# First self attention of a transformer: sixteen piece buffers, two heads built from SBUF, GpSimd as DMA issuer, masked row ahead

## The reference, cut to what matters

```
def _L0_attn_ref(x, wq, wk, wv, wo):
    N_HEADS = 16
    HEAD_DIM = 64
    xq = jnp.einsum('bsh,oh->bso', x, wq)
    xk = jnp.einsum('bsh,oh->bso', x, wk)
    xv = jnp.einsum('bsh,oh->bso', x, wv)
    xq = xq.reshape(bsz, N_HEADS, seqlen, HEAD_DIM)
    scores = jnp.einsum('bhid,bhjd->bhij', xq, xk) * SCALE
    scores = jax.nn.softmax(scores, axis=-1)
    out = jnp.einsum('bhij,bhjd->bhid', scores, xv)
    out = out.reshape(bsz, seqlen, N_HEADS * HEAD_DIM)
    return jnp.einsum('bso,ho->bsh', out, wo)
x = _layernorm(x + _L0_attn_ref(x, wq, wk, wv, wo))
```

## Time and profile before

| what | value |
|---|---|
| median of three runs | 3027.53 us (3024.91 to 3030.15) |
| the profiled execution: its own time | 3025.33 us |
| the profiled execution: its span | 3023.6 us |
| PE busy | 2640.1 us (87%) |
| DVE busy | 1690.4 us (56%) |
| POOL busy | 1567.7 us (52%) |
| ACT busy | 1175.5 us (39%) |
| mean DMA rate | 101 GB/s |

### The profile page before, as it was taken

One profiled execution on the slowest core, in us unless ns is written; L12 is line 12 of the kernel. 1 busy time (PEld: TensorE's weight loads), 2 busy tenths in 40 slices (PEclk: granted clock), 3 DMA queues, 4 the chain that ended last, 5 costly groups with the idle time before them and its releaser, 6 DMA issues. The chain is left out here.

```text
span 3023.6 us, 42611 instructions
## 1 busy us (share of the span) xinstructions
PE 2640.1 (87%) x11953; PEld 1603.7 (53%) x11953; DVE 1690.4 (56%) x3325; ACT 1175.5 (39%) x1640; POOL 1567.7 (52%) x1298
## 2 busy tenths in 40 slices
PE   5999999999999999999999968982795588689696
PEld 4666666666666666666666533431574244334264
DVE  4566666656656566565666535662234455358753
ACT  2444444444444444444444324541222343345334
POOL 0677666776766776676776742224334212222353
PEclk8999999999999999999999979996897599899798
DMA  7545554454545545555454320003893100000143
GB/s 188 119 103 120 113 132 109 112 120 103 120 113 128 112 104 123 112 119 116 111 116 105 75 79 12 2 2 122 343 345 121 39 0 1 29 2 9 33 139 89
DMA packets 406654, 305.26 MB, mean 101 GB/s; under 512 B 291830, under 2 KB 337182, under 8 KB 401438
## 3 DMA queue, kind: packets, MB, share of 16 engines
q1 hardware_dynamic: 390702, 233.93, 33.0%
q0 software_dynamic: 11904, 64.06, 6.0%
q10 hardware_dynamic: 3952, 6.08, 0.6%
HBM read 190.18 MB, written 96.49 MB: 95 GB/s over the span
## 5 line engine op out<-in xcount | busy, mean ns | idle before, releaser
L630 POOL TENSOR_TENSOR a_total<-a_total,a_pr 128x1024 f32<-128x1024 f32 x384 | 915.6, 2384 | 55.8 <-ACT a_pr L614 35.5
L561 DVE TENSOR_REDUCE a_nmax<-a_psX 128x1 f32<-128x512 f32 x1024 | 696.1, 688 | 167.8 <-PE a_psX L556 165.9
L614 ACT ACTIVATE a_pr<-a_psS 128x1024 f32<-128x1024 f32 x512 | 525.3, 1027 | 676.5 <-PE a_psS L602 676.5
L642 PE MATMUL a_psO<-a_pr,a_vd 128*64 128x512 f32 x2048 | 481.8, 602 | 0.0
L556 PE MATMUL a_psX<-a_kA,a_qA 128*128 128x512 f32 x1024 | 411.1, 402 | 30.2 <-DVE a_pl L458 16.2
L630 POOL TENSOR_TENSOR a_total<-a_pr 128x1024 f32<-128x1024 f32 x64 | 153.4, 2398 | 520.2 <-ACT a_pr L614 520.2
L602 PE MATMUL a_psS<-a_qA,a_kA 128*128 128x512 f32 x1024 | 338.4, 412 | 1.6 <-DVE a_nT L577 1.4
L602 PE MATMUL a_psS<-a_qB,a_kB 128*128 128x512 f32 x1024 | 320.4, 394 | 0.7 <-DVE a_qB L585 0.7
L642 PEld LDWEIGHTS a_psO<-a_pr,a_vd 128*64 128x64 f32 x2048 | 129.9, 136 | 236.8 <-issue 179.4
L556 PEld LDWEIGHTS a_psX<-a_kA,a_qA 128*128 128x128 f32 x1024 | 192.9, 189 | 107.5 <-issue 31.8
L602 PEld LDWEIGHTS a_psS<-a_qA,a_kA 128*128 128x128 f32 x1024 | 180.7, 189 | 122.1 <-issue 90.1
(11 more groups left out here) (388 smaller groups left out, 4326.5 us busy)
## 6 DMA issues: line engine op xcount, KB each, us to landing
a_qA<-a_qhi SPq DMA_DIRECT2D x128, 256.0 KB, 4.2
a_qhi<-a_ph SPq DMA_DIRECT2D x128, 128.0 KB, 2.1
a_qlo<-a_pl SPq DMA_DIRECT2D x128, 128.0 KB, 2.2
a_khi<-a_ph SPq DMA_DIRECT2D x128, 128.0 KB, 3.1
a_klo<-a_pl SPq DMA_DIRECT2D x128, 128.0 KB, 2.9
a_kA<-a_khi SPq DMA_DIRECT2D x64, 256.0 KB, 4.0
a_kA<-a_klo SPq DMA_DIRECT2D x64, 256.0 KB, 5.1
a_kB<-a_khi SPq DMA_DIRECT2D x64, 256.0 KB, 5.7
```

What stands on the lines that cost most here:

```text
L561: w.eng.tensor_reduce(nmax[:, half, u:u + 1], psX[:, half, :], AX.X, ALU.max, negate=True)\
L614: w.eng.activation(pr[:, n, :], psS[:, half, :, :].rearrange("p a b -> p (a b)"), ACT.Exp, scale=SCALE)\
L630: w.eng.tensor_tensor(total[:, buf, :], first, pr[:, n, :], ALU.add).then_inc(sems["ad"], 1)
L642: last = w.eng.matmul(psO[q * HD:(q + 1) * HD, :], vd[:, b, kc, :], pr[:, n, q * 512:(q + 1) * 512], start=kc == 0, stop=kc == KC - 1)
```

## The change

Five things are changed in `layer0_self_attention`.

1. `PIECES` goes from 4 to 16: `ph` and `pl` have sixteen buffers, with sixteen semaphores `so0` to `so15`. `build` waits for all of them and for a new one, `sg`.
2. The 16 pieces of group 0 go to DRAM by DMAs that GpSimd issues (32 of them, counted in `sg`), all later pieces by SP as before.
3. The operands of heads 0 and 1 are taken directly from `ph` and `pl` by a new function `build_first`, SBUF to SBUF, in 12 DMAs of 128 KB per head in place of six of 256 KB. ACT waits for these and for `sg` at step 4 of `largest`, before it writes the buffers again.
4. The first weight split stands ahead of the transposition of x.
5. `masked` stands ahead of task "3" at every boundary.

```diff
-    PIECES = 4
+    PIECES = 2 * ROWS // P
...
-        def misc(w, what, G, buf, more=True, bank=None, back=(0, 0)):
+        def misc(w, what, G, buf, more=True, bank=None, back=(0, 0), out="sync"):
...
-                if w.on("sync"):
+                done = f"so{n}" if out == "sync" else "sg"
+                if w.on(out):
...
-                w.inc(f"so{n}", 2 * 16)
+                w.inc(done, 2 * 16)
...
-                w.waits(("s", w.at("s")), *((f"so{n}", w.at(f"so{n}")) for n in range(PIECES)))
+                w.waits(("s", w.at("s")), ("sg", PIECES * 2 * 16), *((f"so{n}", w.at(f"so{n}")) for n in range(PIECES)))
...
+        def build_first(w, j):
+
+            if w.on("sync"):
+                w.wait("md", w.at("md"))
+                for t, rows, src, c, n in ((qA, 0, ph, 0, "a"), (kA, 0, ph, KC, "a"), (qA, HD, ph, 0, "a"), (kA, HD, pl, KC, "a"),
+                                           (kB, HD, ph, KC, "b"), (qB, HD, pl, 0, "b")):
+                    for par in range(2):
+                        w.eng.dma_start(t[rows:rows + HD, j, par * 512:(par + 1) * 512].bitcast(F32).rearrange("p (c t) -> p c t", t=HD),
+                                        src[par * HD:(par + 1) * HD, c:c + KC, j * HD:(j + 1) * HD].bitcast(F32))\
+                            .then_inc(sems[f"f{n}{j}"], 16)
+            w.inc(f"fa{j}", 8 * 16)
+            w.inc(f"fb{j}", 4 * 16)
...
-                rest_first = left > 0 and SLOTS.get((j, "3"), ("T",))[0] in "QK"
-                if more and not rest_first:
+                if more:
                     masked(w, nb)
                 first_d, first_a = under = piece("3")
-                if more and rest_first:
-                    masked(w, nb)
...
             load_x(w, 0)
+            split(0)
             misc(w, ("T",), 0, 0)
...
+                if i in (3, KC):
+                    split((3, KC).index(i) + 1)
+                misc(w, ("QK"[i // KC], i % KC), 0, 0, bank=banks[i % 7], back=(min(i, 6), 0), out="gpsimd")
+            build_first(w, 0)
+            build_first(w, 1)
...
+                if i == 4 and w.on("scalar"):
+                    for n in ("fa0", "fa1", "fb0", "fb1", "sg"):
+                        w.wait(n, w.at(n))
```

More of the change, by code:

```diff
@@ L361, in layer0_self_attention @@
         psM = m.ps("psM", [P, 512])
-        names = ("cst", "cstv", "wq", "wk", "wv", "w", "x", "mi", "md", "ma", "xl", "wh", "wl", "mn", "ch", "a0", "a1", "b0", "b1", "bv", "mx", "mxr", "mt", "mb", "s", "e",
+        names = ("cst", "cstv", "wq", "wk", "wv", "w", "x", "mi", "md", "ma", "xl", "wh", "wl", "mn", "ch", "a0", "a1", "b0", "b1", "fa0", "fa1", "fb0", "fb1", "sg", "bv", "mx", "mxr", "mt", "mb", "s", "e",
                  "ad", "pv", "nm", "rec", "ot", "var", "pl", "rstd", "y", "yo", "dv")
@@ L464, in misc @@
                         w.eng.dma_start(t[bass.ds(row, GH * P), c * HD:(c + 1) * HD].rearrange("(h p) t -> p h t", p=P),
-                                        src[:, n, :].bitcast(F32).rearrange("p (h t) -> p h t", t=HD)).then_inc(sems[f"so{n}"], 16)
-                w.inc(f"so{n}", 2 * 16)
+                                        src[:, n, :].bitcast(F32).rearrange("p (h t) -> p h t", t=HD)).then_inc(sems[done], 16)
+                w.inc(done, 2 * 16)
             elif kind == "V":
@@ L550, in largest @@
                 if i == 0:
+                    w.wait(f"fa{b}", 8 * 16)
                     w.wait(f"a{b}", w.at(f"a{b}"))
@@ L595, in scores @@
                     if kc == 0:
+                        w.wait(f"fb{b}", 4 * 16)
                         w.wait(f"b{b}", w.at(f"b{b}"))
@@ L762, in walk, with split @@
             banks = [psS[:, i // 2, i % 2, :] for i in range(4)] + [psX[:, i, :] for i in range(2)] + [psM[:, :]]
+            def split(n):
+                hi, lo, full = ((wqh, wql, pr[:, 0:2, :]), (wkh, wkl, pr[:, 2:4, :]), (wvh, wvl, total[:, :, :]))[n]
+                if w.on("scalar"):
+                    w.wait(("wq", "wk", "wv")[n], 16)
+                    w.eng.activation(hi[:, :, :], full, ACT.Copy).then_inc(sems["wh"], 1)
+                if w.on("vector"):
+                    w.wait("wh", n + 1)
+                    w.eng.tensor_tensor(lo[:, :, :], full, hi[:, :, :].bitcast(F32), ALU.subtract).then_inc(sems["wl"], 1)
             load_x(w, 0)
+            split(0)
             misc(w, ("T",), 0, 0)
             load_x(w, 1)
-            weights = ((wqh, wql, pr[:, 0:2, :]), (wkh, wkl, pr[:, 2:4, :]), (wvh, wvl, total[:, :, :]))
             for i in range(2 * KC):
[L768 to L779, removed]
+                if i in (3, KC):
[3 more added lines that the diff above has]
+            build_first(w, 1)
             for tt in range(2):
```

## The result

The changed kernel takes 3064.39 us (median of 4 runs, 3062.47 to 3066.36), against 3028.84 us for the kernel before on the same chip (4 runs, 3024.91 to 3037.49). The ratio is 1.011, with an interval of 1.0091 to 1.0129. It is slower by 35.6 us.

A forecast was written before the change was run, and what follows sets the result against it. PE was taken to bound the first self attention. 3025.3 + 34.2 (boundaries) + 5 (start) = 3064.5 profiled, 2.2 below the median, so 3066 against 3027.5; the forecast itself spans 3041 to 3078, the range reaches 3096 with rival B.

The forecast's parts named there:

- rival C: Boundaries between heads: delay partly hidden, half of 34.2, with a start that gains up to 10; 3027 to 3043; 9%.
- A masked row ends a fixed time after the addition, however early it starts: Boundaries after heads 3 and 1: beside a POOL addition, the masked row ends 1.07 to 1.08 us after it.
- 0.95, 0.91 and 0.52 us at the boundaries: Loss per boundary after heads 3, 1 and 0, from the delayed subtraction; 14, 15 and 14 times, 34.2 us.
- Nothing from the sixteen buffers in the loop: Loop: no engine waits for a free buffer, SP's added waits are covered; 0 us, at most 6.
- The start, (1) and (2): Start: wq split before x lands, first piece about 13.0, not 16.36; no landing waits, last rest 29, not 40.2.
- The start, (3): Start: SP issues build_first's eight DMAs for head 0, 0.6 us per 128 KB; first L556 at 36 instead of 52.6.
- The start, (4): Start: ACT waits at step 4 for GpSimd's 32 DMAs, 1.5 us each; scores at 77.3, loss 5.7, rounded to 5.
- a pace of POOL under 1.0 us: Sign at the start: a POOL pace under 1.0 or over 2.0 us per DMA would make the number wrong.
- Rival B: Start: GpSimd's DMAs cost 2.0 to 2.4 us or more, loss 22 to 35 beyond 34.2; 3083 to 3096; 18%.

The follow-up runs named there:

- e3: The changed kernel with GpSimd's last addition of each head cut to 32 of 1024 columns (computes something else, for times alone): 3031.92 us, one run.
- e9: The changed kernel, masked row still ahead, its changed input written to PSUM (bank psO) instead of SBUF: 3030.74 us, ratio 1.0018 to the kernel before.
- e7: The kernel before with PIECES 16 instead of 4 and nothing else: 3027.83 us, ratio 0.9992.
- e6: The changed kernel with the old boundary order; SP sends Q pieces, build_first, then K pieces; ACT's step 4 doesn't await K pieces: 3015.97 us, ratio 0.9953.
- e4: The kernel before with GpSimd's last addition of each head cut to 32 of 1024 columns (computes something else, for times alone): 3028.02 us, one run.

## Why the prediction was right

The forecast was 3066 us and a loss of 1.3%; measured were 3064.39 us and 1.1%. Its own sum, 3064.5 and 2.2, is 3066.7. In rival C, half of 34.2 less a gain of up to 10 gives 3035 to 3045, not 3027 to 3043; that changes nothing in the reading. The boundaries, which make nearly all of the loss, were right in mechanism and some 4 us of 34 too high. The start was near the forecast by luck. The steps, one by one:

- **A masked row ends a fixed time after the addition, however early it starts.** Right: 1.07 and 1.08 us after it in the rows above. e3 and e9 show the cause from two sides: without the addition, or with one input in PSUM, the same instruction takes 1.21 us. The Trainium skill (SBUF — State Buffer, who interferes with whom) says that a DVE operation with two SBUF inputs and a GpSimd operation that reads SBUF lock each other out, and that one with at most one SBUF input, outside the modes that use two ports, does not contend. The traces agree on both sides, 2.59 us against 1.21.
- **0.95, 0.91 and 0.52 us at the boundaries.** L572 or L556 behind `nT` is later by 0.88 after head 3, 0.87 after head 1 (4.30 against 3.42, 3.95 against 3.08, each typical for the loop) and 0.53 after head 0. From one `nT` to the next the loss is smaller where a part is given back inside the next head: 0.81 us in the mean after head 3 (14 heads, 11.4 us), 0.74 after head 1 (14 heads, 10.3 us, between 0.37 and 1.24) and 0.53 after head 0 (14 heads, 7.5 us). So the loop loses 29.3 us, and with the 0.6 after head 1 of group 0 the 43 boundaries of the sum make 29.9 instead of 34.2. What the forecast took for certain, that PE has nothing to give back from, holds for head 0 but not quite for heads 3 and 1.
- **Nothing from the sixteen buffers in the loop.** Right: 106.60 us in e7 against 106.72 for the group of the earlier trace rows, 106.68 against 106.81 in the mean.
- **The start, (1) and (2).** Right: first piece forecast at 13.0 and found at 13.03, last rest forecast at 29 and found at 28.77.
- **The start, (3): first L556 at 36.** Wrong: it is 48.97. The step priced SP's DMAs at 0.6 us each as if they were alone. They cost 0.64 to 0.67 alone (e6: 1.33 for two) and up to 2.3 beside GpSimd's. e6 puts nothing beside them, and L577 starts at 36.55.
- **The start, (4): GpSimd's pace of 1.5 us decides when ACT goes on.** Wrong in both halves. A DMA costs GpSimd 0.75 us, half of the figure taken. The wait of ACT was ended by `build_first`, not by GpSimd's last landing, as the bracket at 61.16 says. That the loss came out near 5 us (1.6 in the scores, 3.2 at the loop's first boundary) rests on two errors of opposite sign: GpSimd was cheaper than taken, and its transfers dearer for the other queue. This is luck. The prediction itself had said that a pace of POOL under 1.0 us would make the number wrong; it was 0.75, and the number held. Nor are the 3.2 us all from the start: they are 1.6 in the scores, 1.6 more in head 0 at the lower granted clock, 0.5 gained in the next head and 0.6 lost at the boundary after head 1. Rival B was written for a high price of issue; its harm came through the other queue's slower transfers instead, and smaller.
- **The sum.** Start 3.2 and loop 29.3 make 32.5 us, the last group adds 1.6, and the unchanged code behind the first attention 4.6; that is the 38.7 between the two profiled spans, where the medians differ by 35.6. The forecast had no term for the 4.6. From the last `nT` of the attention to the end the kernel before takes 1284.1 us and the changed one 1288.7. Among the twelve profiled executions of this document this part ranges from 1283.4 to 1288.7 us, and e4, which has the kernel before's order, buffers and start, also takes 1288.7. So it differs between executions without the change too, and no run ties the 4.6 us to it; what makes this part differ stays open.

## What to carry to other kernels

An instruction that can't finish before another engine's work ends should stand last among the things its engine has to do, not first: moving it up makes it no earlier and holds all that queues behind it. Before moving an issue to an idle engine, ask what its transfers will be beside: the queue whose landing is awaited wants the DMA engines for itself, so putting the transfers in order of need (with a shorter wait of ACT) was worth 8.5 us here, and the choice of issuer lost some 4.5. Where one engine waits for another at SBUF, look whether one operand can sit in PSUM: that was an edit of three lines, and worth some 7 us on top of e6.

## What the runs showed of the hardware that was not expected

- GpSimd spends 0.75 us (0.98 for the first) to issue a DMA of 128 KB with 512 runs of 256 bytes. That is below the 0.97 of its scatters with 128 runs. The Trainium skill (DMA: Bandwidth & Descriptors, Anatomy of one DMA — SWDGE path) holds that many descriptors can be emitted before their number shows in the cost; the trace fits it, though a scatter and a plain DMA are different operations. But the 32nd of them began 8.41 us after the 31st had ended, a wait for nothing that the profile names.
- From GpSimd's queue the same 256 byte runs leave in packets of 2.8 KB, from SP's in packets of 250 bytes. Where both queues were full, the first had 1.32 MB of 1.88 in 10 us. The Trainium skill (DMA: Bandwidth & Descriptors, Queues, rings and completion order) says that the queues take turns at the grain of packets; by that rule the one with larger packets gets more bytes, and the 70% point the same way. They don't show the rule itself: turns of one packet each would make the counts equal, and they were 479 and 2283. What the packets' length depends on was not tried.
- A multiplication of 8 x 1024 with a broadcast input in PSUM runs in 1.21 us beside an addition of POOL in SBUF, the same as without the addition.
